# Plain transposes in place of the centring matmuls, the mean carried as a bias, and an earlier condition for a copy

## The reference

```python
for i in range(DEPTH):                                   # 6
    x = attn_layer(shift_tokens(x), Wqkv[i], ...) + x
    x = ffn_layer(shift_tokens(x), ln_g[i], ...) + x

def ffn_layer(x, g, bln, W1, b1, W2, b2):
    mu = x.mean(-1, keepdims=True)
    var = ((x - mu) ** 2).mean(-1, keepdims=True)
    xn = (x - mu) / jnp.sqrt(var + 1e-05) * g + bln
    a, gate = jnp.split(xn @ W1 + b1, 2, -1)
    return a * gelu(gate) @ W2 + b2
```

## Time and profile before

| | us |
|---|---|
| median of 3 runs | 3763.29 |
| lowest, highest | 3762.48, 3780.51 |
| the profiled execution | 3773.0 |
| its span | 3771.0 |

### The profile page before, as it was taken

One profiled execution on the slowest core, in us unless ns is written; L12 is line 12 of the kernel. 1 busy time (PEld: TensorE's weight loads), 2 busy tenths in 40 slices (PEclk: granted clock), 3 DMA queues, 4 the chain that ended last, 5 costly groups with the idle time before them and its releaser, 6 DMA issues.

```text
span 3771.0 us, 107872 instructions
## 1 busy us (share of the span) xinstructions
PE 3375.2 (90%) x45916; PEld 2204.0 (58%) x46108; DVE 3287.8 (87%) x2914; ACT 2435.9 (65%) x3945; POOL 2810.7 (75%) x1265
## 2 busy tenths in 40 slices
PE   5758999998999999999998999899999999999987
PEld 3325665665665665665666666565666656666664
DVE  6758999998999988999898998898988988998992
ACT  4645766766766766666666676666666666666764
POOL 4457788778787778778777778877777887887771
PEclk9879999999999999999999999999999999999996
DMA  2001111121111111111111111121111111111111
GB/s 72 1 1 36 36 34 38 34 58 41 35 34 39 34 51 44 39 34 35 36 52 44 33 35 35 31 50 44 39 33 34 38 46 45 39 37 35 34 37 36
DMA packets 129694, 141.98 MB, mean 38 GB/s; under 512 B 35388, under 2 KB 73152, under 8 KB 129216
## 3 DMA queue, kind: packets, MB, share of 16 engines
q1 hardware_dynamic: 129216, 135.09, 14.5%
HBM read 19.62 MB, written 2.10 MB: 6 GB/s over the span
## 4 chain that ended last, share of the span: by engine, by line
PE 33%; DVE 23%; POOL 18%; issue 12%; ACT 4%; SPq 3%; DMA 2%; POOLq 0%; ACTq 0%; DVEq 0%
PE bank L570 10%; POOL rr L1138 8%; POOL swp L1148 5%; PE mid L620 4%; DVE Pr L1362 4%; DVE rot L1398 4%; PE mid L579 4%; DVE raw L1390 4%; PE bank L639 4%; PE bank L668 3%; DVE rot L1404 3%; PE mid L607 2%; PE mid L627 2%; DVE ss L1384 2%; PE bank L676 2%
## 5 line engine op out<-in xcount | busy, mean ns | idle before, releaser
L1148 POOL TENSOR_TENSOR swp<-raw,TS 128x1024 f32<-128x1024 f32 x384 | 899.6, 2370 | 622.0 <-DVE raw L1390 622.0
L570 PE MATMUL bank<-wqkv,xs 128*128 128x512 f32 x2304 | 1206.9, 627 | 24.1 <-DMA xs<-F 8.6
L1138 POOL TENSOR_TENSOR rr<-ssm,nhalf 128x32 f32<-128x32 f32 x192 | 1214.8, 6327 | 16.0
L896 ACT ACTIVATE raw<-bank 128x512 f32<-128x512 f32 x768 | 434.6, 592 | 545.0 <-DVE rot L1404 483.8
L579 PEld LDWEIGHTS mid<-ident,rot 128*128 128x128 f32 x3072 | 367.8, 143 | 387.7 <-issue 335.9
L579 PE MATMUL mid<-ident,rot 128*128 128x128 f32 x3072 | 444.6, 278 | 132.7 <-DVE rot L1404 127.3
L1384 DVE TENSOR_REDUCE ss<-sq 128x16 f32<-128x1024 f32 x384 | 463.6, 1207 | 112.1 <-ACT sq L904 111.3
L570 PEld LDWEIGHTS bank<-wqkv,xs 128*128 128x128 f32 x2304 | 387.3, 193 | 289.9 <-issue 194.0
L1390 DVE TENSOR_TENSOR raw<-raw,rr 128x2048 f32<-128x2048 f32 x192 | 469.3, 2444 | 42.6 <-POOL rr L1138 42.6
L1398 DVE TENSOR_TENSOR rot<-raw,TC 128x2048 f32<-128x2048 f32 x192 | 442.2, 2303 | 52.6 <-PE mid L579 51.1
L1404 DVE TENSOR_TENSOR rot<-rot,swp 128x2048 f32<-128x2048 f32 x192 | 440.2, 2292 | 21.0 <-DVE rot L1398 1.4
(11 more groups left out here) (132 smaller groups left out, 4340.8 us busy)
## 6 DMA issues: line engine op xcount, KB each, us to landing
PT<-PTd SPq DMA_DIRECT2D x1344, 64.0 KB
xs<-F SPq DMA_DIRECT2D x192, 64.0 KB, 1.9
BT<-PTd SPq DMA_DIRECT2D x192, 64.0 KB
wqkv<-d_wqkv SPq DMA_DIRECT2D x36, 256.0 KB, 2.8
fwo<-d_fwo SPq DMA_DIRECT2D x6, 512.0 KB, 4.3
d_out<-X SPq DMA_DIRECT2D x8, 256.0 KB, 2.3
w<-d_w SPq DMA_DIRECT2D x6, 341.0 KB
w<-d_w SPq DMA_DIRECT2D x6, 128.0 KB
```

What stands on the lines that cost most here:

```text
L570: nc.tensor.matmul(bank[bk][:, :], xs[:, j, :], wqkv[:, c, :], start=True, stop=True)\
L1138: pool.tensor_tensor(rr[:, :], ssm[:, :], nhalf[:, :], ALU.pow).then_inc(rr_ready, 1)
L1148: last = pool.tensor_tensor(dst[:, :, :, t, :], src[:, :, :, 1 - t, :], tab.unsqueeze(2).broadcast_to([P, 2, HEADS, 32]), ALU.mult)
```

## The change

Three edits.

1. FX is turned to tokens by `nc.tensor.transpose` with the identity instead of the matmul with `cen`. The matrix, its input and its DMA go, and `CONST`, the count of that semaphore, with them.
2. Bank 6 then holds x with its mean. POOL computes `nmean` = -mean and, after the power, `nmr` = rstd * nmean; the copies to `xn` take `nmr` as a bias beside the scale (function Identity in place of Copy). POOL's order in a batch becomes vpe, nmean, rstd, nmr, and `rstd_ready`, on which ACT waits, is now sent by nmr.
3. The first copy of a tile into `raw` waits for the cosine half and the sine half of the tile two before it (`cos_ready`, `sin_ready`) and no longer for their sum.

```diff
-            for dst, src in ((cen[:, :], cen_d), (maskf[:, :, :], mask_d), (tcb, tc_d), (tsb, ts_d),
+            for dst, src in ((maskf[:, :, :], mask_d), (tcb, tc_d), (tsb, ts_d),
...
                 pe.wait_ge(x1_ready, b + 1)
                 for t in range(TPB):
-                    mm = nc.tensor.matmul(bank[6][:, t * P:(t + 1) * P], FX[:, t * P:(t + 1) * P], cen[:, :],
-                                          start=True, stop=True)
+                    mm = nc.tensor.transpose(bank[6][:, t * P:(t + 1) * P], FX[:, t * P:(t + 1) * P], ident[:, :])
                 mm.then_inc(cen_done, 1)
...
                 act.wait_ge(proj_done[c], n + 1)
                 if first:
-                    wait(act, rot_ready, n - 1)
+                    wait(act, sin_ready, n - 1)
+                    wait(act, cos_ready, n - 1)
...
-                    last = nc.scalar.activation(xn[:, t, :], bank[6][:, t * P:(t + 1) * P], ACT.Copy,
-                                                scale=rstd[:, t:t + 1])
+                    last = nc.scalar.activation(xn[:, t, :], bank[6][:, t * P:(t + 1) * P], ACT.Identity,
+                                                scale=rstd[:, t:t + 1], bias=nmr[:, t:t + 1])
...
                 wait(pool, xn_ready, b)
                 pool.tensor_scalar(vpe[:, :], mv[:, :, 1], EPS, None, ALU.add).then_inc(vpe_ready, 1)
                 pool.wait_ge(vpe_ready, b + 1)
-                pool.tensor_tensor(rstd[:, :], vpe[:, :], nhalf[:, 0:TPB], ALU.pow).then_inc(rstd_ready, 1)
+                pool.tensor_scalar(nmean[:, :], mv[:, :, 0], -1.0, None, ALU.mult).then_inc(mean_ready, 1)
+                pool.tensor_tensor(rstd[:, :], vpe[:, :], nhalf[:, 0:TPB], ALU.pow).then_inc(rpow_ready, 1)
+                pool.wait_ge(rpow_ready, b + 1)
+                pool.wait_ge(mean_ready, b + 1)
+                pool.tensor_tensor(nmr[:, :], rstd[:, :], nmean[:, :], ALU.mult).then_inc(rstd_ready, 1)
```

More of the change, by code:

```diff
@@ L56, in tables @@
     return (np.ascontiguousarray(c, np.float32), np.ascontiguousarray(s, np.float32),
-            np.ascontiguousarray(m, np.float32), np.eye(P, dtype=np.float32),
-            (np.eye(P) - 1.0 / D).astype(np.float32))
+            np.ascontiguousarray(m, np.float32), np.eye(P, dtype=np.float32))
 def wait(eng, sem, value):
@@ L69, in adaln_block @@
                 wqkv_d, qks_d, fwo_d, g_d, bln_d, w1_d, b1_d, w2_d, b2_d,
-                tc_d, ts_d, mask_d, eye_d, cen_d, out_d):
+                tc_d, ts_d, mask_d, eye_d, out_d):
     ctx = ExitStack()
@@ L82, in adaln_block @@
         ident = sb("ident", [P, P])
-        cen = sb("cen", [P, P])
         identb = sb("identb", [P, P], BF16)
@@ L134, in adaln_block @@
         rstd = sb("rstd", [P, TPB])
+        nmean = sb("nmean", [P, TPB])
+        nmr = sb("nmr", [P, TPB])
         xn = sb("xn", [P, TPB, P])
@@ L266, in adaln_block @@
         rstd_ready = sem("rstd_ready")
+        rpow_ready = sem("rpow_ready")
+        mean_ready = sem("mean_ready")
         xn_ready = sem("xn_ready")
@@ L308, in adaln_block @@
         FWL = 12 * 16
-        CONST = 5 * 16
+        CONST = 4 * 16
         def layer(n):
@@ L1482 @@
     f = lambda name: np.asarray(inputs[name])
-    tc, ts, mask, eye, cen = tables()
+    tc, ts, mask, eye = tables()
     arrays = {
@@ L1492 @@
         "w2": f("L0_ffn_W2"), "b2": f("L0_ffn_b2").reshape(DEPTH, 1, D),
-        "tab_cos": tc, "tab_sin": ts, "mask": mask, "eye": eye, "cen": cen,
+        "tab_cos": tc, "tab_sin": ts, "mask": mask, "eye": eye,
     }
```

## The result

The changed kernel is slower: 3842.57 us in the median of four runs (3830.61 to 3845.72) against 3766.91 (3762.48 to 3780.51, four runs) of the kernel before, a ratio of 1.0189 with a 95% interval of 1.0153 to 1.0224. The forecast was 3842. The profiled execution took 3830.6, with a span of 3828.8; before it was 3773.0 and 3771.0. The granted clock of the span is 0.953, where it was 0.962. Three executions in the experiments, one each of the kernel before and of the first and the third edit alone, took 5744 to 11963 us and are left out of every ratio.

A forecast was written before the change was run, and what follows sets the result against it. No engine is full (PE 90%, DVE 87% busy), so instruction order decides. Early batches 45, late 13 and clock 21 make 79 on the profiled 3773.0, 3852, or 3842 on the median; range 3795 to 3890.

The forecast's parts named there:

- The ring of DVE and POOL: Chain `normed`, `swp`, `probs`: DVE products and POOL instructions hold each other; `swp` 1.3 later makes the next cosine 1.3 later.
- the power held to the end of `normed`: On POOL, `nmean` makes the power start 0.06 behind DVE's `normed` instead of 0.17 ahead, held until 930.70.
- early batch: Batch whose `ssm` starts ahead of DVE's cosine; 32 of 48, each to pay 1.4, 45 in all.
- Both paths end together: The `swp` path and the path over the `xn` copies and PE both delay the next cosine by 1.3.
- Late batches: Batches whose `ssm` is held beside DVE's cosine; 16 of them, each to pay 0.8, 13 in all.
- The clock: PE's longer idle time before `xn` lowers its clock in 13 early batches at 1.6 each, 21 in all.
- The fall behind the first idle time fills the second: A clock fall after PE's wait for `rot` costs nothing: the lost time goes into the 2.8 idle before L658.
- the rival of a fall behind L659 in every early batch: PE's clock falls behind its wait for `xn` in all early batches: 51 instead of 21, 3872; chance 0.12.
- Centring 0: Transposes save PE 0.5 a batch, up to 27, but only lengthen its idle time before `rot`: counted at 0.
- raw copies 0: ACT's copies to `raw` go up to 2.3 earlier, but PE still waits for `rot`: counted 0, other end -58.
- The rival asked for a `nmean` of under 0.1: The power still starts ahead of `normed`; an early batch pays only the bias: 19 in all, 3783; chance 0.07.
- The two rivals about the mix: Late batches turn early, 3721, chance 0.05; or early turn late, 3873 for eight, 3967 for all, chance 0.06.

The follow-up runs named there:

- one more instruction: Kernel before plus only `nmean` on POOL ahead of the power, its output unused, no `nmr` or bias: ratio 1.0101 to before.
- `nmean` on DVE: Changed kernel with `nmean` moved from POOL to DVE, behind its statistics: ratio 1.0084 to the kernel before.
- power first: Changed kernel with the power and `nmean` exchanged on POOL, so the power comes straight behind `vpe`: ratio 1.0155 to the kernel before.
- the filler: Changed kernel with eight identity transposes on PE into bank 7 just before its wait for `xn`: ratio 1.0149 to the kernel before.

## Why the prediction was right, point by point

**The ring of DVE and POOL, and the power held to the end of `normed`: right, in size too.** 1.4 was forecast for an early batch, and the slots without a fall behind L659 went from 17.50 to 18.89. But the step on which it all hangs had less room than its working says. The power was to start at the end of `nmean`, 0.06 behind `normed`; it starts 0.18 after `nmean` does (1600.02, 1600.20) and comes 0.01 to 0.02 behind. In all thirteen traces together, every start of `ssm`, `rr`, `vpe`, `nmean` or the power that lies 0.04 to 0.5 ahead of DVE's cosine, sum of the halves or `normed` was free, every one level with it or up to 0.3 behind was held, and between 0.01 and 0.03 ahead both happened. That the power fell on the held side by so little is luck.

The way from there to the slot can be checked on five kernels. Let r be the time from the cosine to the end of what releases ACT's copies to `xn` (the power, or `nmr`), in one batch of each; the slot is that of the common kind, without a fall:

| kernel | r | slot | slot - r |
|---|---|---|---|
| before | 9.02 | 17.50 | 8.48 |
| one more instruction | 11.32 | 18.25 | 6.93 |
| `nmean` on DVE | 10.71 | 18.02 | 7.31 |
| power first | 10.87 | 18.17 | 7.30 |
| after | 11.59 | 18.89 | 7.30 |

Three kernels with the bias agree within 0.01, and the one without it is 0.37 below them, which is what the bias costs: the group of four copies takes 1.51 after and 1.13 in the earlier trace rows. So in all four the slot hangs on ACT's release; before, 1.55 of slack lay behind it (8.48 - 6.93). 2.57 + 0.38 - 1.55 = 1.40.

**Three sizes inside that were off.** The bias was put at 0.2 and costs 0.38; I had its price from copies of another shape, of which moreover the one with the bias reads PSUM and the other SBUF. The start of the copies was put 2.2 later and came 2.05 later (11.63 after the cosine, 9.58 in the earlier trace rows). The two errors cancel, which is luck. The delay of `swp` was put at 1.3. It is 11.55 after the cosine where it was 10.51, so 1.04 later. "Both paths end together" was therefore wrong: the path over ACT and PE ends last. On it L659 came 2.42 later, as forecast (13.28 after the cosine; the earlier trace rows give 10.86), and 1.03 of that was slack, where 1.1 was forecast.

**Late batches: the delay right, the price not.** From the cosine to L658 or L659 the late batches took 15.02 in the mean before and 15.79 after, 0.77 more, and 0.8 was forecast. But the slot grew by 0.43 only, since what follows got shorter, 7.84 to 7.51. One late batch after (cosine at 1155.50, next at 1178.45) on PE:

```profile
1171.21 1.09 PE L659 MATMUL bank<-ident,xn 128*128 128x128 f32 x4 [5.37 <-ACT xn L982]
1172.09 1.91 PE L572 MATMUL bank<-wqkv,xs 128*128 128x512 f32 x2
...
1174.65 1.97 PE L641 MATMUL bank<-OT,fwo 128*128 128x128 f32 x16
```

All of this but the last row is at the lower level. Before, the same group (L639) took 2.40 in the batch of the earlier trace rows. A later start may leave less work for the stretch at the lower level. Whether it is that or chance, with six of the sixteen late batches exchanged, the runs don't tell: the kernel with the third edit alone has L658 at 14.99 and 7.49 behind it, in 14 batches that scatter from 6.91 to 8.42. The 16 x 0.37 = 6 are small beside the rest.

**The clock: right in kind and price, the number a guess.** 13 falls behind L659 at 1.6 were forecast; 11 came, and a fall costs 1.59 to 1.62 in five kernels (20.50 against 18.89, 19.77 against 18.17, 19.60 against 18.01, 20.47 against 18.85, 19.87 against 18.25). The share of 4 in 10 had no row behind it, so that it came near is luck. "The fall behind the first idle time fills the second" holds throughout: in the 28 early batches with a held power the clock fell just once. In 17 it fell in the first idle time, and PE then waited 1.50 to 1.56 for `xn` and kept its clock; in the other 11 it stayed up there, PE waited 2.17 to 3.20, and it fell. So the rival of a fall behind L659 in every early batch did not come. What decides in the first idle time is open, and the length alone does not settle it: 2.13 was followed by a fall in the batch shown above, and the same 2.13 in another batch of that execution (L581 at 719.14) by four passes at 1.88. Nor does it behind the wait for `xn`: in the kernel with the filler the clock fell after 2.01 and stayed after 2.02 and 2.23.

**Centring 0 and raw copies 0: right.** Each was run by itself, at 0.9962 and 0.997. Neither changed the mean early slot by more than 0.09. Their ratios are worth 14 and 11 us, which the sum did not have; they go with 12 and 14 late batches instead of 16, and shorter ones.

**The other rivals.** The power got in ahead of `normed` in two batches of 46: in one `rr` started 0.04 ahead of the cosine, took 5.46 and ended early, in the other `normed` itself came 0.36 later. The rival asked for a `nmean` of under 0.1; by the starts above, some 0.05 less between `nmean` and the power would have been enough in every batch, so it was nearer than its chance of 0.07 says. The two rivals about the mix both happened, six batches each way, and cancelled: 30 to 16 both times. That nothing in the change delays FX, or pulls it forward, did not keep single batches from turning, so that the count stayed is partly luck too. In the early batches of both traces `ssm` is 0.05 to 0.41 ahead of the cosine. What one batch is worth is near what was written: 5.4 before (22.87 - 17.50), and 3.9 after (23.30 - 19.45).

**The sum.** 79 was forecast on the profiled execution and 57.6 came. By terms: early without falls 30 x 1.40 = 42 (45 forecast); falls 11 x 1.6 = 18 (21); late 7 (13); other slots -6 (0). That makes 61; of the 3 too many 1 is the slots at 17.60, 18.18 and 21.56, and 2 are what a count of 46 of 48 batches leaves out. Between the medians the 75.7 are near the 79, but that the number 3842 was met so closely is partly luck: the execution in the profile was the fastest of its four, that of before 6 above its median. One more late batch costs 3.9 in the changed kernel and 5.4 before, and the ranges, 15 and 18 us wide, are no more than three or four of them. That such batches make the scatter from run to run is likely and was not looked at, since each kernel has one trace here.

**Open.** What decides in the kernel before which batch is late (the start of `ssm` follows FX, and that a chain from the block DMAs) was not tested. Why the other three slots of a batch lost 0.13 after the change was not either; three single slots now took 20.4.

## What to carry to other kernels

Look for the small instruction that just gets in ahead of a long one on another engine: how much of a new neighbour it can bear is the gap between the two starts (0.17 here), and its price is what is left of the long one, not its own length (0.23 of work held the next instruction for 2.1). Before adding to such a place, move something out of it: the `ssm` taken from POOL was worth more than any of the three edits. And an idle time of PE that grows, here from 0.39 to 2.25, can have a second price, the clock (1.6 a fall), which shows only where the work behind it has no slack.

## What the hardware showed that I had not expected

- The hold works one way for the power. `normed` took 2.28 beside a power that had started 0.17 before it, and the cosine 2.28 beside an `rr` that had started 0.11 before it and still ran for 5.43. But an `rr` that starts 0.09 behind the cosine takes 7.49, and a power of four numbers 0.01 behind `normed` 3.16. With `swp` DVE is held: `probs` took 2.33 beside it and 1.22 when it had ended. The Trainium skill (SBUF — State Buffer, "SBUF: two separate sides") has the first to start keep the ports for its whole instruction; all runs bear that out for POOL behind DVE, none for DVE behind a power.
- Less than a tenth of a microsecond decides: starts of POOL 0.01 and 0.02 behind DVE's were held to its end, those 0.09 and 0.11 ahead were free. The edge lies just ahead of level: before the change an `ssm` at 1339.82 took 2.42 though the cosine started at 1339.84, and after it one 0.05 ahead (3281.92) took 0.30.
- Four 128x128 copies with a column of scale and one of bias took 1.51, with a scale alone 1.13.
- Transposes with the identity of the same 128x128 blocks took 30.2 where matmuls took 54.1, each of them standing as one record where the matmul has two.
